# Stage borders, router logits and projection order of a six-layer float32 decoder kernel

## What is computed

```python
logits = xf @ gate_w.T + gate_b
logits = logits * jax.lax.rsqrt(ms + eps) * rms_w      # ms: mean square
g = top_1(softmax(logits / 0.5));  norm_g = g / (g + 1e-6)
h = gelu(einsum('nd,edh->neh', xf, w1) + b1)
out = ((einsum('neh,ehd->ned', h, w2) + b2) * norm_g[:, None, None]).sum(axis=1)
```

## Time and profile before

| | |
|---|---|
| median of 3 runs | 1612.79 us (1612.34 to 1615.42) |
| the profiled execution, its own time | 1614.47 us |
| span of its trace, first to last instruction | 1612.7 us |
| mean granted TensorE clock | 0.98 of full speed |
| busy share | PE 96%, PEld 83%, DVE 62%, ACT 43%, POOL 13% |
| instructions | 28704 |
| DMA | 66.5 MB, mean 41 GB/s |
| the chain that ended last | PE 87%, DVE 7%, DMA 2%, issue 2%, ACT 1% |

### The profile page before, as it was taken

The page is one execution under the profiler, slowest core; times in us unless marked ns, Lnnn a source line. Parts: engine busy times, 40 slices in busy tenths (PEclk is TensorE's granted clock), DMA queues, the critical chain, the costliest instruction groups (busy, mean ns, idle before and its releaser), DMA issues.

```text
span 1612.7 us, 28704 instructions
## 1 busy us (share of the span) xinstructions
PE 1544.3 (96%) x11112; PEld 1332.9 (83%) x11112; DVE 997.2 (62%) x2133; ACT 686.3 (43%) x1807; POOL 202.7 (13%) x214
## 2 busy tenths in 40 slices
PE   6999999899999999989999899999988999999997
PEld 5888888689899899978888677777766988888896
DVE  6777776845554545575666568788865464444446
ACT  1544554522221222222233277788864444444443
POOL 1222222310000000020000113212221300000001
PEclk9999999999999999989999999999989999999999
DMA  6000100001010101000000376687830000000001
GB/s 210 2 15 1 41 2 1 27 25 39 15 51 27 50 26 38 23 10 33 1 33 1 44 120 88 87 104 130 101 66 27 1 26 27 27 26 17 35 0 52
DMA packets 43065, 66.51 MB, mean 41 GB/s; under 512 B 4560, under 2 KB 33488, under 8 KB 42832
## 3 DMA queue, kind: packets, MB, share of 16 engines
q1 hardware_dynamic: 42960, 65.09, 20.0%
HBM read 36.24 MB, written 2.10 MB: 24 GB/s over the span
## 4 chain that ended last, share of the span: by engine, by line
PE 87%; DVE 7%; DMA 2%; issue 2%; ACT 1%; SPq 1%; POOL 0%; DVEq 0%; POOLq 0%; ACTq 0%
PE ps L85 22%; PE ps L87 21%; PE ps L86 21%; PE ps L1660 3%; PE ps L1674 2%; PE ps L373 2%; PE ps L397 2%; PE ps L1650 2%; PE ps L1705 2%; PE ps L384 2%; PE ps L1688 1%; PE ps L367 1%; PE ps L1647 1%; DMA nQs<-nQc_h 1%; SPq L1500 1%
## 5 line engine op out<-in xcount | busy, mean ns | idle before, releaser
L795 ACT ACTIVATE m2hT_h<-ps 128x512 fp32r<-128x512 f32 x128 | 76.7, 599 | 285.7 <-PE ps L87 285.7
L914 DVE TENSOR_TENSOR m6hT_l<-m6h,m6hT_h 128x512 fp32r<-128x512 f32 x128 | 88.5, 692 | 174.4 <-ACT m6hT_h L793 174.3
L916 DVE SCALAR_TENSOR_TENSOR m2hT_l<-ps,m2hT_h 128x512 fp32r<-128x512 f32 x128 | 88.5, 691 | 161.7 <-ACT m2hT_h L795 161.7
L792 ACT ACTIVATE m6h<-ps,m6b 128x512 f32<-128x512 f32 x128 | 88.3, 690 | 207.4 <-PE ps L87 192.2
L1781 ACT ACTIVATE nPr<-ps,negm 128x128 f32<-128x128 f32 x512 | 147.2, 383 | 28.7 <-DVE negm L1878 28.0
L87 PE MATMUL ps<-w_h,m6hT_l 128*128 128x256 f32 x512 | 144.9, 283 | 0.0
L85 PE MATMUL ps<-w_h,m6hT_h 128*128 128x256 f32 x512 | 143.9, 281 | 1.0 <-DVE m6hT_l L914 1.0
L86 PE MATMUL ps<-w_l,m6hT_h 128*128 128x256 f32 x512 | 144.2, 282 | 0.0
L87 PE MATMUL ps<-m2w_h,m2hT_l 128*128 128x256 f32 x448 | 126.8, 283 | 0.0
L86 PE MATMUL ps<-m2w_l,m2hT_h 128*128 128x256 f32 x448 | 126.7, 283 | 0.0
L85 PE MATMUL ps<-m2w_h,m2hT_h 128*128 128x256 f32 x448 | 126.3, 282 | 0.0
(11 more groups left out here) (288 smaller groups left out, 4358.4 us busy)
## 6 DMA issues: line engine op xcount, KB each, us to landing
nKm<-nKc_h SPq DMA_DIRECT2D x64, 128.0 KB, 4.6
nQs<-nQc_h SPq DMA_DIRECT2D x64, 128.0 KB, 5.9
raw<-in_w_e1i SPq DMA_DIRECT2D x9, 512.0 KB, 3.3
raw<-in_w_e1o SPq DMA_DIRECT2D x9, 512.0 KB, 3.4
raw<-in_w_e6i SPq DMA_DIRECT2D x9, 512.0 KB, 3.3
raw<-in_w_e6o SPq DMA_DIRECT2D x9, 512.0 KB, 3.5
raw<-in_w_a SPq DMA_DIRECT2D x8, 512.0 KB, 4.6
nKm<-nKc_l SPq DMA_DIRECT2D x32, 128.0 KB, 5.2
```

The costliest lines, as they stand in the source:

```text
L792: nc.scalar.activation(c.h32[:, u % 2, :], ps[:, u % 2, :], ACT.Gelu, bias=bias)
L795: nc.scalar.activation(c.hT[0][:, ch, :], ps[:, u % 2, :], ACT.Relu).then_inc(c.s["hi_ready"], 1)
L914: last = nc.vector.tensor_tensor(c.hT[1][:, ch, :], c.h32[:, u % 2, :], c.hT[0][:, ch, :].bitcast(F32), ALU.subtract)
L916: last = nc.vector.scalar_tensor_tensor(c.hT[1][:, ch, :], ps[:, u % 2, :], 0.0, c.hT[0][:, ch, :].bitcast(F32), ALU.max, ALU.subtract)
```

## The change

The diff shows every part that the prediction speaks of; "..." marks what is left out.

**First attention.** V of a group is projected in the first two of its own pairs (`w_of_step`: four lists, the places of the fills within a step), x has two slots, `w_start` keeps only x, q and k of group 0. q, k and v units now hold 512 outputs with both halves of the features (`halved`), so fills 0 and 1 of q need unit 0 alone. `cols` has its own semaphore and is loaded ahead of unit 1. ACT makes the high parts of units 1 to 5 (`A1_BY_ACT`), DVE the low ones; units 6 and 7 are split beside fills of step 2. Gates are taken three pairs later. The transposes of x for M2 stand in steps 30 to 35 instead of 28 to 33.

```diff
-    def w_fills(G):
-        return [(kind, (G, j)) for kind in "qkv" for j in range(4)] + ([("x", (G + 1, 0))] if G + 1 < NGW else [])
...
+    def w_of_step(p):
+
+        G, k = divmod(p, 4)
+        if G >= NGW:
+            return [[], [], [], []]
+        own, later = [("v", (G, j)) for j in range(4)], G + 1 < NGW
+        q, key = ([(kind, (G + 1, j)) for j in range(4)] if later else [] for kind in "qk")
+        return ([own[0:1], own[1:2], [("x", (G + 1, 0))] if later else [], []],
+                [own[2:3], own[3:4], q[0:1], q[1:2]],
+                [q[2:3], q[3:4], [], []],
+                [key[0:1], key[1:2], key[2:4], []])[k]
+
+    def w_start():
+        return [("x", (0, 0))] + [(kind, (0, j)) for kind in "qk" for j in range(4)]
...
-    W_X_AT, W_U_AT, W_W_AT = 28, NP, (28, 30)
+    A1_BY_ACT = (1, 2, 3, 4, 5)
+    W_X_AT, W_U_AT, W_W_AT = 30, NP, (28, 30)
...
-            w, unit = (w_q, 2) if kind == "q" else (w_k, 4)
-            if G == 0 and j == 0:
-                pe.wait_ge(prep_done, U_A1 + unit)
+            w, unit = (w_q, 0) if kind == "q" else (w_k, 2)
+            xh, xl = W.XT[G % 2]
+            if G == 0 and j % 2 == 0:
+                pe.wait_ge(prep_done, U_A1 + (unit + 1 + j // 2))
...
-            if p % 4 == 0:
-                pe.wait_ge(s["g_evac"], w_fill(G, "k", 3) + 1)
             if p > 0:
                 pe.wait_ge(s["p_exp"], 2 * p)
             for half in range(2):
                 nc.tensor.matmul(ps[:, WSB[half], :], identb[:, :], causal[:, :, :].rearrange("p a b -> p (a b)"),
                                  start=True, stop=False)
+            if p % 4 == 0:
+                pe.wait_ge(s["g_evac"], w_fill(G, "k", 3) + 1)
...
+        for k in A1_BY_ACT:
+            act.wait_ge(raw_loaded[k % 2], (U_A1 + (k - k % 2)) * 8 + 16)
+            nc.scalar.activation(wA1[0][:, k * RAW:(k + 1) * RAW], raw[k % 2][:, :], ACT.Identity).then_inc(split_act, 1)
...
-                if p < NP:
-                    gates_of(p, part)
+                if 0 <= p - 3 < NP:
+                    gates_of(p - 3, part)
```

```diff
+            for u in range(NU):
+                up(i, u)
+                down(i, u - 2)
+        i = E_OUT // 2
+        down(i, -2)
+        if between:
+            between()
+        down(i, -1, halves=c.gelu)
...
-                if u >= HC + 2 and u % HC == 2:
+                if u % HC == 2:
                     combine(i, u // HC - 1)
                 weights(i, u)
-            combine(i, 2 * NG - 1)
...
+        combine_half(0)
+        stats_half(0)
+        combine_half(1)
+        stats_half(1)
+        normalise_half(0)
+        normalise_half(1)
...
                     router(g)
+                    if type(g) is int and g == 0:
+                        of_mixture[0]()
                 elif kind == "t":
                     product(g, c)
+                    if type(g) is int and g == 0 and c == 1:
+                        of_mixture[1]()
+                        v.sem_inc(stage_done, 1)
```

```diff
+            rows_hl, rows_h = ps[0:2 * E_OUT, 5, :], ps[0:E_OUT, 5, :]
+            nc.tensor.matmul(rows_hl, both[0], c.XT[0][:, g, 0, :], start=True, stop=False)
+            for i in range(DC):
+                nc.tensor.matmul(rows_h, gw[:, i, 0, :], c.XT[1][:, g, i, :], start=False, stop=False)
+            nc.tensor.matmul(rows_hl, both[1], c.XT[0][:, g, 1, :], start=False, stop=True).then_inc(c.s["logits"], 1)
...
-            order += n_quad("t", n, 2) + n_quad("s", n) + n_seq("ze", n, 5) + n_seq("zt", n, 8) + n_fill_of(n)
-            order += ([("me", 0)] if n == NQUADS - NQ + M_E_AT else []) + n_following(n, 1)
+            order += n_quad("t", n, 2) + n_quad("s", n)
+            order += ([("me", 0)] if n == NQUADS - NQ + M_E_AT else []) + (n_following(n, 1) if n >= NQUADS else [])
+            order += n_seq("ze", n, 5) + n_seq("zt", n, 8) + n_fill_of(n) + (n_following(n, 1) if n < NQUADS else [])
...
-    M_X_AT, M_L_AT, M_U_AT, M_D_AT = (6, 7, 8, 9, 13, 14), (10, 11, 15), (16, 17, 18, 19), (20, 21)
-    M_G_AT, M_E_AT = (12, 13, 17), 16
+    M_X_AT, M_L_AT, M_U_AT, M_D_AT = (6, 7, 8, 9, 14, 15), (10, 11, 16), (16, 17, 18, 19), (20, 21)
+    M_B_AT, M_G_AT, M_E_AT = (12,), (12, 13, 17), 16
```

More of the change, by code:

```diff
@@ L422, in w_tensor @@
                     transpose_p(2 * (p - 2) + half)
-                for kind, i in f[half:half + 1]:
+                for kind, i in f[half]:
                     fill(kind, i)
@@ L426, in w_tensor @@
                 out_project(b)
-            for kind, i in f[2:3]:
+            for kind, i in f[2]:
                 fill(kind, i)
@@ L430, in w_tensor @@
                 values(p - 2)
-            for kind, i in f[3:]:
+            for kind, i in f[3]:
                 fill(kind, i)
@@ L764, in down, with mix_tensor @@
                               skip_group_check=True)
-            if ch == HC - 1:
+                if halves and j % 2 == 1:
+                    last.then_inc(c.s["half_full"], 1)
+            if ch == HC - 1 and not halves:
                 last.then_inc(c.s["d_full"], 1)
-        return {"x": transposed_x, "l": logits, "u": up, "d": down}
-    def mix_tensor(pe, c, parts):
+        return {"x": transposed_x, "l": logits, "b": logits_back, "u": up, "d": down}
+    def mix_tensor(pe, c, parts, between=None):
         for kind, k in mix_order(c):
-            if kind in "xl":
+            if kind in "xlb":
                 parts[kind](k)
@@ L1741, in n_tensor @@
                 after["l"](i)
+            elif kind == "mb":
+                after["b"](i)
             elif kind == "md":
```

299 lines of the change are left out of this document (180 added, 119 removed).

## The result

The changed kernel took **1590.66 us** (median of 4 runs, 1586.64 to 1591.46), the kernel before 1612.57 us on the same chip (median of 4, 1609.45 to 1615.42): ratio 0.9862, 95% interval 0.984 to 0.9884. The forecast was 1587 with a range of 1577 to 1597. The profiled execution took 1589.92 us, span 1588.1 (before 1614.47 and 1612.7), so the two traces differ by 24.5 us; the prediction's sum was 26.1.

| Stretch | sum predicted | measured |
|---|---|---|
| start, up to the first scores | 11.1 | 11.6 |
| steps 0 to 3 | -1.1 | -1.1 |
| steps 4 to 27, six groups of four | 0 | **-7.2** |
| steps 28 to M2's first down | -1.2 | 0.0 |
| M2, first down to last | 0.7 (loops) | 0.4 (loops 1.1, F3's transposes of x, now ahead of the last down, -0.7) |

A forecast was written before the change was run, and what follows sets the result against it. PE, busy 96%, bounds the kernel; only its idle time, half-clock matmuls and both ends can be won. 8.8 + 4.2 + 6.5 + 5.4 + 1.2 = 26.1 us off 1614.47, 1.7 less for the median: 1587, range 1577 to 1597.

The forecast's parts named there:

- M2 to F3: Border of M2 and F3: gain 6.5 us, leaning on the router's 2.70 us instruction shrinking; 4 if it stays.
- Start: First attention's start: PE begins at 8.65, scores at 25.7 instead of 36.8 us, 11.1 us sooner.
- The rival that loads bind the start: Start of first attention: units land later than 4.6 us, gain 3 instead of 8.8, total 1592 us; chance 0.13.
- Steady part: First attention's steady steps: K evacuation wait costed at nothing; without cover 0.7 at 7 borders, 5 us.
- Parts 1 to 3: First attention's start, steady steps and tail together: 8.8 us gained, bounds 5 and 12.
- the "slower" rival: Steady steps: PE waits for DVE's V and K evacuations in each of 28; at 1.6 us each 1632 us; chance 0.03.
- Tail: End of first attention: step 28 takes 9.5 us, step 29 6.5; x's transposes return in steps 34 and 35, +1.2.
- N to M6: Border of N and M6: 4.0 - 2.2 + 3.6 = 5.4 us gained from logits and table load; bounds 1 and 8.
- The half-clock rival: Step 29, behind M2, before M6: PE's new short waits keep stretches at 1.2 GHz; sum 17, total 1596 us; chance 0.12.
- M6's loops: M6's loop borders: a down between two ups removes PE's four low-part waits, 3.9 us in all; 3.5 us taken.
- End: Kernel's end: last normalising and store in halves, 0.5 + 0.7 = 1.2 us gained; bounds 0.3 and 2.
- All bounds half used: Whole kernel: with all bounds half used, the forecast case reaches from 1579 to 1594 us.

The follow-up runs named there:

- run 4: The changed kernel with each pair's token gates in its own step again (0 instead of 3 later): 1597.68 us, ratio 0.9905.
- Runs 1 and 2: Changed kernel with K fills one to a place (1583.52 us, ratio 0.9832); with every K fill one place sooner, 2 and 3 still together (1582.24 us, 0.9803).
- run 6: The changed kernel with POOL's memset of nKm right behind M2's last combine instead of behind product 1: 1593.61 us (one run).
- run 9: The changed kernel with M6's logits in the old form (x as the weights, no transposes back): 1591.91 us, ratio 0.9873.
- run 8: The changed kernel with ScalarE's old order at N to M6 (an up's activation behind the step's copies): 1595.63 us, ratio 0.9887.

## Why the prediction was right, and where it was not

The time was right within 4 us, and so were the start, M2 to F3 and the end. But four terms were off by 1.7 to 7.2 us, two each way (-7.2 and -2.0, +4.3 and +1.7), and that they nearly cancelled is luck: the 4.3 us stand in no part of the prediction.

- **Start: right.** PE began at 8.50 (8.65 said), the first scores at 25.18 (25.7), ScalarE's high part took 1.06 (1.1). The rival that loads bind the start fell. Not seen: the start stands on the gates' lag (run 4, 7 us), which the prediction costed as "The gates only move". It asked what DVE's work hides, not when the gates' operands land against scores that come 11 us sooner.
- **Steady part: the step that failed.** "The new order puts the K evacuation ahead of the values and the mask ..., so I cost that wait at nothing." That looked at the scores, who wait for K fill 3. The wait was within the fills: fill 3 needs the bank of fill 1, whose evacuation stands behind half the gates and the norm chain. The price, six waits of 0.86 to 0.91 us in steps 4 to 27, 5.3 us, lies by the bound that the prediction had named and set aside (5 us without cover), and with 0.3 per group that are no single wait it came to 7.2. Parts 1 to 3 gave 3.4 us instead of 8.8, outside their bounds of 5 to 12. Runs 1 and 2 show it: with every K fill one place sooner they cost nothing. It is the "slower" rival's mechanism at a sixth of its size (7.2 us against 28 times 1.6), since it bit once in four steps and not in each.
- **Tail:** steps 28 and 29 as worked out (9.34 and 6.48 us, 9.5 and 6.5 said); behind them 1.0 us better than the sum.
- **M2 to F3: right in size**, 6.2 in the table for 6.5, or 5.5 when F3's transposes, now ahead of M2's last down, are counted as the prediction did. Two errors met: PE waited 2.9 us and not 3.9, but the logits' end and the first up ran at half clock (0.51 from 704.0 to 707.4), where the sum had full clock. The router's 2.70 us went because the memset no longer ran over it; run 6 brings them back as 3.92. No run undoes the rest of this order, or M2's loops; their gains are read from the two traces alone.
- **N to M6: right for the table load, wrong for the logits.** The sum gave the new form 4.0 less 2.2. Up to up 0 it brought -0.5, and run 9 finds no difference. The wait ahead of the transposes back was as forecast (2.13 for 2.2). The term that failed is the gain of 4.0: it was taken from the 9.5 us of before, in which two groups ran partly at half clock; the old form in run 9 takes 7.4, so the form itself saves 2.4, and the longer wait ahead of the third group (1.36 us) was not in the sum.
- **Not in the sum:** 4.3 us between up 3 and up 8. 1.0 of it is the l 3 wait, which came back with ScalarE's old order. The rest is clock: this stretch ran at 0.87 before and at 1.00 after,

```profile
1235.74:1261.29 25.55, 23.10 (x135) 20.82 (x133) 14.12 (x32) 8.65 (x14) 4.18 (x6) 0.87 0.13 42
```

```profile
1221.89:1243.15 21.26, 19.81 (x130) 17.23 (x129) 13.23 (x26) 8.64 (x14) 2.50 (x4) 1.00 0.16 50
```

  and at 1.00 in run 8 too, with the old wait in it. So the 3.3 us are not tied to that wait; what else lifted them stays open. The same holds for the 1.3 us won at F3 to N, where the granted clock went from 0.78 (909.28 to 940.62 us before) to 0.89 (900.13 to 930.13).
- **The half-clock rival** (0.12) came true in kind at both borders and in full at one: M2 to F3 went from 0.78 to 0.90, with 3.4 us at half clock left, N to M6 only from 0.83 to 0.86 (0.92 in other runs of the same code). The page "TensorE: Matmul & The Clock Gate" of the Trainium skill, that transposes do not count as activity, could not be tested: run 9 does without the transposes back, and its 0.83 against 0.86 is a smaller difference than this stretch shows with no edit at all.
- **M6's loops:** 5.2 for 3.5. The 3.9 us were the waits alone; a border costs 0.4 us beyond its wait.
- **End: right**, 1.2 us.
- **Two slips in its numbers.** "All bounds half used" gives 1583 at the fast end, for the bounds of parts 1 to 7 lie 6.9 us above the sum together; 1579 needs all of them. And the chances of the forecast and the rivals add up to 1.02.

## What to carry to other kernels

Where fills share two banks, ask for each fill who holds its bank and what stands ahead of that evacuation on its engine, and not only whether the last one is in time; moving the K fills by one place was worth 6 to 8 us here. When a stage starts sooner, check the landing time of every operand that it and its side work read. Judge each part of a bundle by undoing it alone: one of the six here cost 3 us, one was worth nothing, and one that looked like bookkeeping carried 7.
